# Fourth stage: the rank term as one product of 26 stacked rows in split f32r parts

## What is computed

```
def _sage(x, adj, Wr, Wx, b, mf):
    deg = clip(sum(adj, -1), 1)
    out = (adj @ x / deg) @ Wr + x @ Wx + b
    return out / max(norm(out), 1e-12) * mf

h1 = bn(relu(sage(x,  adj_d, Wr1, Wx1, b1)))
h2 = bn(relu(sage(h1, adj_d, Wr2, Wx2, b2)))
h3 = bn(relu(sage(h2, adj_d, Wr3, Wx3, b3)))
x + (concat(h1, h2, h3) * mf @ Wl + bl) * mf
```

## Time and profile before

| | us |
|---|---|
| median of three runs (2792.62 to 2796.52) | 2793.79 |
| the profiled execution | 2807.94 |
| its span | 2805.9 |
| PE busy, share of the span | 2676.0, 95% |
| DVE busy | 2195.6, 78% |
| ACT busy | 1274.3, 45% |
| POOL busy | 1090.1, 39% |
| fourth stage in that execution, about | 2583 to 2765 |

### The profile page before, as it was taken

One profiled execution on the slowest core, in us unless ns is written; L12 is line 12 of the kernel. 1 busy time (PEld: TensorE's weight loads), 2 busy tenths in 40 slices (PEclk: granted clock), 3 DMA queues, 4 the chain that ended last, 5 costly groups with the idle time before them and its releaser, 6 DMA issues. The chain is left out here.

```text
span 2805.9 us, 41224 instructions
## 1 busy us (share of the span) xinstructions
PE 2676.0 (95%) x13446; PEld 1690.8 (60%) x13446; DVE 2195.6 (78%) x5582; ACT 1274.3 (45%) x3780; POOL 1090.1 (39%) x493
## 2 busy tenths in 40 slices
PE   6999999999989999999999978999999879999997
PEld 4666666666656656666666644555555545555886
DVE  5789999999879988999998968666666336774667
ACT  2555645665444454656554302333333324443665
POOL 3635344400143455730000007766666304342661
PEclk9999999999999999999999989999999989999998
DMA  6465374462273384572151123555555129996552
GB/s 231 150 214 185 108 215 152 124 216 74 78 246 113 113 285 143 160 230 83 57 188 59 35 80 143 201 201 201 201 201 199 55 105 396 396 395 241 215 201 121
DMA packets 322365, 491.76 MB, mean 175 GB/s; under 512 B 20576, under 2 KB 214496, under 8 KB 322144
## 3 DMA queue, kind: packets, MB, share of 16 engines
q1 hardware_dynamic: 322144, 489.05, 50.9%
HBM read 421.86 MB, written 67.11 MB: 174 GB/s over the span
## 5 line engine op out<-in xcount | busy, mean ns | idle before, releaser
L600 POOL TENSOR_SCALAR a_T<-stage 128x512 uint8<-128x512 f32 x256 | 513.4, 2013 | 713.3 <-DMA stage<-in_adjT 711.0
L680 PE MATMUL a_acc<-a_ew,a_Hr 128*128 128x512 f32 x1536 | 761.4, 603 | 0.0
L861 DVE TENSOR_TENSOR a_ew<-adj,a_cos 128x512 f32<-128x512 f32 x768 | 505.4, 679 | 39.7 <-PE a_cos L673 38.4
L671 PE MATMUL a_cos<-a_nh 128*128 128x512 f32 x768 | 408.2, 532 | 3.6 <-DVE a_nl L853 2.6
L1469 POOL TENSOR_TENSOR b_dsum<-adj 128x1024 f32<-128x1024 f32 x16 | 136.5, 8534 | 600.4 <-DVE adj L1419 600.4
L680 PEld LDWEIGHTS a_acc<-a_ew,a_Hr 128*128 128x128 f32 x1536 | 269.0, 190 | 140.2 <-issue 104.8
L786 ACT ACTIVATE a_vr<-a_D,a_small 128x128 f16<-128x128 f32 x560 | 210.5, 457 | 256.1 <-DVE a_small L931 255.9
L796 ACT ACTIVATE a_v<-a_D,a_wb,a_small 128x256 f16<-128x256 f32 x512 | 260.7, 562 | 120.2 <-PE a_D L714 108.2
L673 PE MATMUL a_cos<-a_nh,a_nl 128*128 128x512 f32 x768 | 304.0, 396 | 0.0
L672 PE MATMUL a_cos<-a_nl,a_nh 128*128 128x512 f32 x768 | 301.9, 393 | 0.0
L1473 POOL TENSOR_TENSOR b_dsum<-b_dsum,adj 128x1024 f32<-128x1024 f32 x96 | 229.8, 2394 | 14.4 <-POOL b_dsum L1473 0.9
(11 more groups left out here) (226 smaller groups left out, 4554.2 us busy)
## 6 DMA issues: line engine op xcount, KB each, us to landing
adj<-in_adjT SPq DMA_DIRECT2D x108, 1024.0 KB, 12.7
adj<-in_adjT SPq DMA_DIRECT2D x128, 512.0 KB, 4.6
stage<-in_adjT SPq DMA_DIRECT2D x256, 256.0 KB, 3.2
stage<-in_adj SPq DMA_DIRECT2D x256, 256.0 KB, 3.8
scr_keep<-a_kp SPq DMA_DIRECT2D x256, 64.0 KB, 1.5
stage<-scr_keep SPq DMA_DIRECT2D x13, 1024.0 KB, 7.6
c_zi<-scr_z SPq DMA_DIRECT2D x26, 512.0 KB, 6.1
c_ai<-scr_ag SPq DMA_DIRECT2D x20, 512.0 KB, 7.3
```

The source lines that it names most:

```text
L600: e.tensor_scalar(TT[:, Q * (quad % 2) + i, 4 * h:4 * h + 4, blk(k)].bitcast(U8), ats[h], 0.0, ONE8, ALU.is_gt, ALU.mult).then_inc(T["at"], 1)
L671: e.matmul(cos[j][:], n[:, blk(k)], n[:, half(j)], start=True, stop=False)
L680: e.matmul(acc[j][:], Hr[u % 2][:, k, :], ew[idx % EW][:], start=(k == 0), stop=(k == NK - 1)).then_inc(E["agg"], 1)
L861: e.tensor_tensor(ew[idx % EW][:], adj[g % 2][:, k, half(j)], cos[j][:], ALU.mult).then_inc(E["ew"], 1)
```

## The change

The rank term's products take f32r operands (fp32 words read by PE at reduced precision) with 26 rows in place of fp32 ones with 9. To keep precision, each factor is split in a rounded part and the rest: rho = rh + rl, p = ph + pl, b = bh + bl. The rows of the stationary operand are rho (rounded, 8 rows), rl (8), rho again (rounded, 8) and two of ones; those of the moving one are, in block k, ph, ph, pl, bh and bl. The product rl * pl is left out.

- `setup` adds on DVE two selection tiles `sel` (26x8) and `own` (26x2), made from the identity by four reductions and an addition, behind a wait for the identity.
- Two tiles are added in front of the large ones, `rho3`, `krow` and `rhoT` grow; scratch space is taken from `o[1]`.
- Ahead of the graphs, DVE builds `rho3` (128 x 16 x 26) and the 26-row `krow`. PE's first transpose waits for `rho3`.
- Per graph, `turn_rho` transposes 26 columns in place of 8 and ACT copies 26x128 in place of 8x128. The two products of the rank term keep their lines and their waits.

```diff
+RANKS = 3 * NK + 2
+        C["sel"], C["own"] = sb("sel", [RANKS, NK]), sb("own", [RANKS, 2])
 def setup(nc, A, C):
+            e.wait_ge(S["ident"], 1)
+            rest, diag = P.sb("rest", [RANKS, 1]), C["ident"][0:RANKS]
+            e.tensor_reduce(rest[:], diag[:, 3 * NK:RANKS], AXX, ALU.add).then_inc(S["sums"], 1)
+            e.tensor_reduce(C["sel"][:], diag[:, 0:3 * NK].rearrange("p (r k) -> p k r", k=NK), AXX, ALU.add).then_inc(
+                S["sums"], 1)
+            e.tensor_reduce(C["own"][:, 0:1], diag[:, 0:2 * NK], AXX, ALU.add)
+            e.tensor_reduce(C["own"][:, 1:2], diag[:, 2 * NK:3 * NK], AXX, ALU.add)
+            e.wait_ge(S["sums"], 2)
+            e.tensor_scalar(C["sel"][:], C["sel"][:], rest[:, 0:1], None, ALU.add).then_inc(S["sel"], 1)
 def layer1_third(nc, A, C, S):
-        rhoT = [P.sb(f"rhoT{i}", [NK + 1, 128]) for i in range(2)]
-        krow = P.sb("krow", [NK + 1, NK, 128])
+        rhoT = [P.sb(f"rhoT{i}", [RANKS, 128], F32R) for i in range(2)]
+        rho3 = P.sb("rho3", [128, G, RANKS], F32R)
+        krow = P.sb("krow", [RANKS, NK, 128], F32R)
+        bh, ph = (o[1][0:RANKS, i, :].bitcast(F32R) for i in range(2))
+        bl, pl, mix = (o[1][0:RANKS, i, :] for i in range(2, 5))
...
-                e.transpose(pt[0:NK, 0, :], C["rho"][:, n, :], C["ident"][:]).then_inc(E["tr"], 1)
+                else:
+                    e.wait_ge(E["split"], 4)
+                e.transpose(pt[0:RANKS, 0, :], rho3[:, n, :].bitcast(F32), C["ident"][:]).then_inc(E["tr"], 1)
...
-                e.activation(rhoT[n % 2][0:NK, :], pt[0:NK, 0, :], ACT.Copy).then_inc(E["rho"], 1)
+                e.activation(rhoT[n % 2][:], pt[0:RANKS, 0, :], ACT.Copy).then_inc(E["rho"], 1)
...
-            for i in range(2):
-                t = e.memset(rhoT[i][:], 1.0)
-            t.then_inc(E["ones"], 1)
-            e.tensor_copy(krow[:], ...)
-            e.tensor_tensor(krow[0:NK], ...)
+            b, p, diag = C["rows"][0:RANKS, 5, :], C["rows"][0:RANKS, 6, :], C["ident"][0:RANKS]
+            e.tensor_copy(rho3[:, :, 0:NK], C["rho"][:]).then_inc(E["split"], 1)
+            e.tensor_copy(ph, p).then_inc(E["vh"], 1)
+            e.tensor_copy(bh, b).then_inc(E["vh"], 1)
+            e.tensor_copy(rho3[:, :, 2 * NK:3 * NK], C["rho"][:]).then_inc(E["split"], 1)
+            e.wait_ge(E["split"], 1)
+            e.tensor_tensor(rho3[:, :, NK:2 * NK], C["rho"][:], rho3[:, :, 0:NK].bitcast(F32), ALU.subtract).then_inc(
+                E["split"], 1)
+            e.memset(rho3[:, :, 3 * NK:RANKS].bitcast(F32), 1.0).then_inc(E["split"], 1)
+            e.wait_ge(E["vh"], 2)
+            e.tensor_tensor(pl, p, ph.bitcast(F32), ALU.subtract).then_inc(E["vl"], 1)
+            e.tensor_tensor(bl, b, bh.bitcast(F32), ALU.subtract).then_inc(E["vl"], 1)
+            e.tensor_scalar(mix, ph.bitcast(F32), C["own"][:, 0:1], None, ALU.mult).then_inc(E["vb"], 1)
+            e.wait_ge(E["vl"], 1)
+            for i, (v, weight) in enumerate(((pl, C["own"][:, 1:2]), (bh.bitcast(F32), diag[:, 3 * NK:3 * NK + 1]),
+                                             (bl, diag[:, 3 * NK + 1:RANKS]))):
+                e.wait_ge(E["vl"], 2)
+                e.wait_ge(E["vb"], i + 1)
+                e.scalar_tensor_tensor(mix, v, weight, mix, ALU.mult, ALU.add).then_inc(E["vb"], 1)
+            e.wait_ge(E["vb"], 4)
+            e.tensor_tensor(krow[:], mix.unsqueeze(1).to_broadcast([RANKS, NK, 128]), bc(C["sel"][:], 128),
+                            ALU.mult).then_inc(E["krow"], 1)
```

More of the change, by code:

```diff
@@ L158, in setup @@
         P = Scope(nc, ctx, "s", C["bank"][1])
-        S = P.sems("mask ident low upper mine fills")
+        S = P.sems("mask ident low upper mine fills sums sel")
         mi = P.sb("mi", [128, 128], I32)
@@ L1668, in layer1_third @@
         E = P.sems("zi0 zi1 zi2 ai0 ai1 ai2 yi0 yi1 xi0 xi1 nz ny tz zt bs pr1 pr2 py c f sq cl nrm rn rm zr"
-                   " pb tb px out kbias krow ones tr rho")
+                   " pb tb px out vh vl vb split krow ones tr rho")
         zT, part = C["z3"], [p.rearrange("p (k d) -> p k d", d=128) for p in C["part"]]
@@ L1760, in rho @@
                 e.wait_ge(E["tr"], n + 1)
-                if n == 0:
-                    e.wait_ge(E["ones"], 1)
                 if n > 1:
                     e.wait_ge(E["pr2"], n - 1)
-                e.activation(rhoT[n % 2][0:NK, :], pt[0:NK, 0, :], ACT.Copy).then_inc(E["rho"], 1)
+                e.activation(rhoT[n % 2][:], pt[0:RANKS, 0, :], ACT.Copy).then_inc(E["rho"], 1)
             rho(0)
```

## The result

The changed kernel took 2789.24 us (median of 16 runs, 2785.87 to 2800.67), the kernel before 2797.57 in the same comparison (16 runs). The ratio is **0.9967, 95% interval 0.9957 to 0.9978**: between 6 and 12 us faster. In the profiled executions the fourth stage, from its first transfer's issue to the first instruction of `final`, went from 181.8 us (2583.03 to 2764.87) to 170.9 (2572.97 to 2743.89), 10.9 us less. The rest of the 20 us between the two spans (2805.9 and 2785.4) lies almost wholly ahead of the stage (10.1 us at its start, 10.0 of them already where the second network begins).

What follows compares the result with a forecast made beforehand. PE was taken as the bound, then the loop through DVE's addition at 9.51 us per graph. Gains of 1.0 and 10.1 less 0.1 make 11.0 us: 2796.9 for the profiled execution, 2782.8 as median, range 2775.5 to 2789.5.

Steps and rivals of the forecast that it cites:

- The loop behind PE: Fourth stage, per graph: copy, DVE's addition, `py`, transposes, next copy take 9.51 us; 0.72 of 1.21 us is won.
- The product: Rank term on PE, per graph: slot falls from 1.91 to 0.70 us, saving 1.21; PE alone would need 9.03.
- ACT's slack: Fourth stage, per graph: ACT's wait for PE's transposes falls from 1.20 to about 0.5 us.
- PE's idle time: Fourth stage: PE stands idle some 0.5 us at `py` in every graph, until DVE's addition is done.
- The clock: Rival: PE's idling lowers its granted clock to half in a third of the graphs; +32 us, 2826; chance 5%.
- the rule cited for it: Trainium skill, TensorE page: frequent micro-idling between product groups can make PE's clock swing between its levels.
- The transpose and copy of rho: Per graph, 26 columns transposed and 26x128 copied beside `py` work: nothing to 0.1 us on ACT, taken as zero.
- The preparation: DVE ahead of the first graph: `krow` ready 2.3 us later, but PE's next group starts 0.2 us early (-0.6 to +0.6).
- The start: Graph 0's addition hangs on POOL and transfers and stays where it was; 1.0 us won in graph 1 (0.3 to 2.1).
- the lock rival: DVE's L1813 held by POOL's lock ends behind the moments' start: period 9.9, gain 5.0 us, 2788.8; chance 14%.
- the forecast left 0.5: Steady part: DVE's L1813, held until POOL's operation ends, still ends 0.5 us ahead of the moments and costs nothing.
- The sum: 1.0 us in graph 1, 10.1 in graphs 2 to 15, 0.1 less in the last period: 11.0 us.

Runs made afterwards that it cites:

- e1: Changed kernel with DVE's moments of graph n-1 moved from ahead of the addition of graph n to behind it; median 2779.93 against 2789.98 us.
- e3: Changed kernel with the two rank products of every graph issued twice; 2789.32 against 2789.98 us, period 9.58 unchanged.
- e6: Changed kernel with the two rank products of every graph issued three times; ratio 0.9988 to the kernel before, period 9.91 us.
- e7: Changed kernel with DVE's moments moved behind the addition and the two rank products issued twice; ratio 0.9946 to the kernel before, period 9.45 us.
- e5: Kernel before with only the setup's two small tiles and five small DVE operations added, unused; ratio 0.9996 to the kernel before.
- e0: Changed kernel without an edit, timed again as base for the others; ratio 0.9972 to the kernel before, period 9.58 us.
- e4: Changed kernel with the two rank products reading the same 26-row operands as fp32; ratio 1.0011 to the kernel before, 11.3 us above the unedited changed kernel.

## Why the prediction was right

**The loop behind PE** was the step that decided, and it held. Forecast 9.51 us, measured 9.58. Its parts: copy to `py` 4.83 (4.76 forecast), `py` to transposes 3.57 (3.57), transposes to copy 1.18 (1.18). The missing 0.07 is the hand-over from DVE's addition to PE's weight load, 0.11 us here (2649.72 to 2649.83), for which I took the 0.05 of the earlier trace rows. e1 shows by removal, e3, e6 and e7 by added work, that this wait and nothing else takes the other half of what PE saved.

**The product.** Slot 0.66 us, forecast 0.70; PE alone 8.98 (e1), forecast 9.03. As said, the exact price didn't matter.

**ACT's slack** is 0.55 us, forecast 0.5. **PE's idle time** is 0.37 us per graph in its own rows, forecast some 0.5. **The clock** stayed at 1.00 in the steady part with PE idle in each graph; that rival and the rule cited for it have no row for them here. **The transpose and copy of rho** cost nothing to be seen.

**The preparation** on DVE took from 2573.01 to 2577.05, 4.04 us, forecast 4.4; the next group's start, 5.34 us into the stage for 6.01 before, was 0.7 us earlier where 0.2 was forecast:

```profile
2573.01 0.23 DVE L1812 CAST c_rho<-rho 128x128 fp32r<-128x128 f32 x1 [0.81 <-PEq L86]
...
2575.84 1.21 DVE L1831 TENSOR_TENSOR c_krow<-c_o,sel 26x1024 fp32r<-26x1024 f32 x1
...
2577.20 1.19 PE L1740 MATMUL c_p<-c_krow,c_rhoT 26*128 26x512 f32 x2 [2.88 <-DVE c_krow L1831]
...
2578.31 3.78 PE L1745 MATMUL c_p<-W,stage 128*128 128x128 f32 x16
...
2581.89 2.28 PE L1752 MATMUL c_p<-W,h 128*128 128x128 f32 x16
...
2587.07 0.48 DVE L1841 TENSOR_SCALAR c_rns<-c_rnss 128x8 f32<-128x8 f32 x1 [0.70 <-ACT c_z L1792]
...
2587.60 2.35 POOL L1878 TENSOR_TENSOR adj<-adj,c_tb 128x1024 f32<-128x1024 f32 x1
...
2588.06 1.92 DVE L1849 TENSOR_TENSOR c_rm<-c_rnrn,mf 128x8 f32<-128x8 f32 x1
...
2590.05 2.16 DVE L1853 SCALAR_TENSOR_TENSOR adj<-c_py,mf,adj 128x128 f32<-128x128 f32 x8
```

**The start was mis-sized.** I left graph 0's addition where it was. It came 1.6 us earlier (17.08 us into the stage, 18.71 before), and the first copy 2.6 us. Before, the clamp L1813 came behind the start of POOL's long addition and took 1.98 us. The multiplication L1821 behind it then took 0.65 us and ended with POOL's next operation. Now the clamp came 1.5 us earlier: it ended 0.05 us before POOL's long addition started, and only the following L1849 stood behind POOL (it ends at 2589.98, POOL at 2589.95). Of these 1.5 us, 0.7 are the earlier start of PE's first group behind the product, and 0.9 the clock, which rose 2.5 us earlier than in the profile of before, during PE's second group. The prediction had named this ("if the clock rises at another moment than before, 1.5 us either way") and put it at nothing. The same group in before and, with the same stage, in e5:

```profile
2592.61 3.15 PE L1736 MATMUL c_p<-W,h 128*128 128x128 f32 x16
```

```profile
2592.36 1.97 PE L1747 MATMUL c_p<-W,h 128*128 128x128 f32 x16
```

With the early clock the first copy of e5 comes 1.2 us earlier than in before. So up to 1.2 of the 2.6 us may not be the change's; no run settles it. The term isn't stable otherwise, either: over the profiles with the old stage the first copy came after 25.5 to 26.7 us, over the three with the new product once per graph, all with the early clock, after 24.1 to 25.4.

**A small loss that I had not seen** is in the last graph, whose period is 10.22 in place of 9.58:

```profile
2722.57 2.36 POOL L1878 TENSOR_TENSOR adj<-adj,c_tb 128x1024 f32<-128x1024 f32 x1
...
2724.15 0.80 DVE L1849 TENSOR_TENSOR c_rm<-c_rnrn,mf 128x8 f32<-128x8 f32 x1
2724.87 2.15 DVE L1853 SCALAR_TENSOR_TENSOR adj<-c_py,mf,adj 128x128 f32<-128x128 f32 x8
```

L1849 ends at 2724.95 and POOL's operation at 2724.93. Without transfers to wait for, POOL's last addition comes earlier and meets the multiplication on DVE's path: the lock rival, in one graph, for 0.6 us. e0 and e3 show the same (L1849 takes 0.74 and 0.79 us there), e7 more of it (1.97 us). The section "SBUF: two separate sides" of the Trainium skill's page "SBUF — State Buffer" counts a DVE operation with two inputs in SBUF among those that the lock concerns, against a POOL operation that reads SBUF; L1849 and L1878 are such a pair, and both rows agree. In the steady part L1841 ended with POOL's operation (2654.47 and 2654.45) and 1.2 us ahead of the moments, where the forecast left 0.5.

**The sum.** First copy 2.6, 13 periods x 0.65 = 8.4, last graph -0.1: 10.9 us, forecast 11.0. That the two agree to 0.1 us is luck: the start was put 1.6 us too small, the 13 periods together 0.9 too large and the last graph 0.7 too large. The measured ratio is 8 to 9 us rather than 11, which its interval holds. The start may be part of the difference: in the repeat e0 it gained 1.9, the stage 10.3, and against e5's stage of before (180.6) e0's is 9.1 us shorter. The rest is not settled. The absolute forecast of 2782.8 rested on the 2793.79 of three runs; the kernel before came out at 2797.57 over 16, which is most of why 2789.24 lies at the upper edge of the range, 0.3 us inside it (e0, the same kernel, took 2789.98). What held is the mechanism and, within its interval, the difference; the absolute time was met narrowly.

## What to carry to other kernels

A full engine doesn't say how much of a saving will come out: before shortening it, write down every loop that passes through it, with what each wait on that loop has to spare (here 0.72 of 1.21 us, measured 0.65 of 1.25). The loop that then binds may have work in it that doesn't belong to it; moving it behind (here the moments, behind the addition) was worth as much as the change itself, and without the change only some 1 us in the tail. How much idle time the shortened engine really has can be measured: add work to it until the period moves (here 0.6 us per graph). And a sum that comes out right can hold terms that don't: here the start and the last graph were off in opposite directions.

## What the runs showed of the hardware

- An f32r product of 26x512 costs what one of 128x512 does: a pair adds 0.47 us to the slot in e3 and to the period in e7, 0.23 each. An fp32 product is two records 0.43 us apart, with 26 rows as with 9 (e4).
- The hand-over from DVE to a PE weight load that is already held up took 0.11 us (2649.72 to 2649.83), twice the 0.05 us of the kernel's start.
- A DVE operation on 128x8 elements that took 0.17 us in the steady part (L1849) took 1.92 us beside a POOL operation of 2.35 us, and ended 0.03 us behind it. In the changed kernel, e0 and e1 this POOL operation starts 14.6, 15.3 and 15.9 us into the stage, because the transfer for POOL's second operation landed at different times (that operation starts after 6.4, 7.1 and 7.6 us). L1849 ends with it each time, and the first copies follow after 24.1, 24.8 and 25.4 us.
- The granted clock rose from 0.50 to 1.00 between 9.6 and 13.0 us into the stage. Two profiles of the same stage code differ by 2.5 us in it (12.1 in before, 9.6 in e5), and the first copy by 1.2 us.
